# Normalised rows of a macaron layer: split on GpSimd and transposed by the DMA engines instead of TensorE, with two feed-forward layers a step earlier

## What is computed

```python
def ffn(x):                      # weights are +1 or -1, from boolean tables
    h = concat([x, -x])          # 256
    h = 2 * relu(s0 * h @ w(k0)) # 512
    h = 2 * relu(s1 * h @ w(k1)) # 512
    return s2 * h @ w(k2)        # 128

def attn(x):                     # 16 heads of 8
    q, k, v = x @ Wq.T + bq, x @ Wk.T + bk, x @ Wv.T + bv
    ctx = softmax(q @ k.T / sqrt(8)) @ v
    return layernorm(ctx + x) * gamma + beta

x = x + 0.5 * ffn(ln(x))
x = x + attn(ln(x))
x = x + 0.5 * ffn(ln(x))
```

## Time and profile before

| | us |
|---|---|
| median of three runs | 745.43 (744.24 to 748.4) |
| profiled execution, its own time | 745.53 |
| span from first to last instruction | 743.7 |

### The profile page before, as it was taken

How to read it: one execution, slowest core, us unless ns; L and a number is a source line. 1 busy time by engine, 2 the same in 40 slices (tenths; PEclk the granted TensorE clock), 3 DMA queues, 4 the chain that set the end, 5 groups by cost and what they waited for, 6 DMA issues and landing times.

```text
span 743.7 us, 18698 instructions
## 1 busy us (share of the span) xinstructions
PE 695.9 (94%) x7347; PEld 336.0 (45%) x7347; DVE 649.1 (87%) x1270; ACT 510.4 (69%) x745; POOL 365.9 (49%) x650
## 2 busy tenths in 40 slices
PE   7878999999999999999999999999999998787887
PEld 3434344544444454444444444444445444342346
DVE  6687898989999899999989898999989898887766
ACT  3426777777777777777787777767777776766644
POOL 6532455574454647454463746445465745254330
PEclk9999999999999999999999999999999999999999
DMA  3101010201102020201102020110201001010000
GB/s 82 57 15 52 16 53 2 65 17 45 37 3 66 17 66 16 67 17 29 39 16 66 16 66 17 44 38 2 67 17 65 17 33 36 30 38 2 11 7 30
DMA packets 29527, 25.65 MB, mean 34 GB/s; under 512 B 4353, under 2 KB 29441, under 8 KB 29441
## 3 DMA queue, kind: packets, MB, share of 16 engines
q1 hardware_dynamic: 27824, 23.74, 10.0%
q10 hardware_dynamic: 1616, 0.72, 0.3%
HBM read 5.05 MB, written 4.19 MB: 12 GB/s over the span
## 4 chain that ended last, share of the span: by engine, by line
PE 70%; DVE 20%; issue 4%; ACT 3%; POOL 2%; DMA 1%; SPq 0%; DVEq 0%; POOLq 0%
PE ps_c L876 15%; PE ps_z L702 13%; PE ps_z L703 11%; DVE row_max L1507 9%; PE ps_s L823 9%; DVE ffn_lo L1382 6%; PE ps_z L692 3%; PE ps_z L693 3%; PE ps_z L684 2%; PE ps_m L808 2%; PE ps_m L797 2%; ACT ffn_hi L1117 2%; PE ps_c L797 2%; PE ps_z L713 2%; DVE k_lo L1498 1%
## 5 line engine op out<-in xcount | busy, mean ns | idle before, releaser
L1507 DVE TENSOR_REDUCE row_max<-ps_s 128x4 f32<-128x1024 f32 x256 | 312.3, 1220 | 31.0 <-PE ps_s L823 29.3
L1156 ACT ACTIVATE probs<-ps_t,score_scale 128x1024 f32<-128x1024 f32 x252 | 280.2, 1112 | 62.2 <-PE ps_t L836 59.6
L1117 ACT ACTIVATE ffn_hi<-ps_z 128x512 f16<-128x512 f32 x261 | 149.8, 595 | 80.1 <-PE ps_z L703 63.2
L702 PE MATMUL ps_z<-ffn_hi,w 128*128 128x512 f16 x464 | 177.1, 382 | 0.8
L703 PE MATMUL ps_z<-ffn_lo,w 128*128 128x512 f16 x464 | 175.9, 379 | 0.0
L1382 DVE SCALAR_TENSOR_TENSOR ffn_lo<-ps_z,ffn_hi 128x512 f16<-128x512 f32 x232 | 154.3, 684 | 20.3 <-ACT ffn_hi L1117 17.4
L876 PE MATMUL ps_c<-probs,v_cols 128*32 128x256 f32 x2048 | 131.9, 386 | 1.3 <-ACT probs L1156 0.7
L823 PE MATMUL ps_s<-k_rows,q_rows 32*128 32x256 f16 x1024 | 100.2, 273 | 14.8 <-DVE row_max L1507 12.7
L836 PE MATMUL ps_t<-q_rows,k_rows 32*128 32x256 f16 x992 | 97.1, 273 | 0.0
L876 PEld LDWEIGHTS ps_c<-probs,v_cols 128*32 128x32 f32 x2048 | 57.0, 109 | 54.3 <-issue 26.6
L823 PEld LDWEIGHTS ps_s<-k_rows,q_rows 32*128 32x128 f16 x1024 | 29.0, 92 | 103.8 <-issue 50.4
(11 more groups left out here) (223 smaller groups left out, 1101.6 us busy)
## 6 DMA issues: line engine op xcount, KB each, us to landing
x<-L_attn_x SPq DMA_DIRECT2D x16, 256.0 KB, 2.7
q_rows<-q_hi SPq DMA_DIRECT2D x32, 128.0 KB, 2.5
k_rows<-k_hi SPq DMA_DIRECT2D x31, 128.0 KB, 2.1
y<-x SPq DMA_DIRECT2D x15, 256.0 KB, 2.2
q_rows<-no_max SPq DMA_DIRECT2D x16, 128.0 KB, 2.2
q_rows<-q_lo SPq DMA_DIRECT2D x16, 128.0 KB, 2.2
k_rows<-k_lo SPq DMA_DIRECT2D x15, 128.0 KB, 2.1
q_rows<-max_rows SPq DMA_DIRECT2D x64, 8.0 KB
```

Of the source, the lines that this page charges most:

```text
L702: pe.matmul(o[:], w, ffn_hi[:, 1 + k, :], start=(k == 0), stop=False)
L1117: a_.activation(ffn_hi[:, use, :], ps_z[use % 2][:], ACT.Relu if use else ACT.Copy, scale=1.0 if use else XN_SCALE).then_inc(z_hi, 1)
L1156: a_.activation(probs[n % PROBS][:, j:j + 2, :], o[:], ACT.Exp, scale=score_scale[:, 0:1]).then_inc(s_exp, 1)
L1507: v.tensor_reduce(row_max[hb % 2][:].rearrange("p (a l) e -> p l a e", a=2)[:, j:j + 2, :, g % 2], ps_s[:].rearrange("p l (a k) -> p l a k ...
```

## The change

The rows of 26 feed-forwards (all but feed-forward 0 and those of the last two iterations; the solo ones stay as well) and of the attention of tiles 1 to 15 are no longer transposed by TensorE. GpSimd multiplies the centred rows by a scaled factor twice, once to half precision and once to full, subtracts, and so has the `hi` and the `lo` rows side by side in `ffn_rows` or `att_rows` (128 partitions x 1024 half-precision elements, 256 KB). SP issues one transposing transfer to `ffn_cols` or `att_cols`. These feed-forwards have nine uses of `ps_z` instead of ten, and their pieces of the first and middle layer stand one step earlier; the last layer keeps its steps. The query projection goes from step 8 to 11, the key projection from 11 to 13. Statistics of `ffn_a` are finished at step 7 instead of 10, those of `next_b` at 26 instead of 27, those of the attention at 27 instead of 26. `tail_base` follows the first `split_max` instead of preceding it.

```diff
-AT = {"LNT": 6, "Q": 8, "K": 11, "CT0": 14, "CT1": 22, "V": 25}
+AT = {"Q": 11, "K": 13, "CT0": 14, "CT1": 22, "V": 25}
-AT_STATS_A, AT_STATS_B, AT_STATS_PREP = ((2, 2, 9, 9), 10), ((24, 24, 25, 25), 27), ((18, 18, 20, 20), 26)
+AT_STATS_A, AT_STATS_B, AT_STATS_PREP = ((2, 2, 6, 6), 7), ((24, 24, 25, 25), 26), ((18, 18, 20, 20), 27)
...
+FFN_IN_SOON = {1: 0, 2: 1, 3: 2, 4: 3}
+FFN_MID_SOON = tuple((5 + n, 2 * n, 2 * n + 2) for n in range(8))
+FFN_MID_DONE_SOON = {6: 0, 8: 1, 10: 2, 12: 3}
...
+        FFNS_ON_PE = (0, second_ffn(T - 4), second_ffn(T - 3))
+
+        def by_dma(f):
+
+            return f not in FFNS_ON_PE
...
+            def turn_ffn(f):
+
+                sp.wait_ge(z_full, z_use(f - 1, 5))
+                sp.wait_ge(f_xn, f + 1)
+                sp.dma_start_transpose(ffn_cols[:], ffn_rows[:].rearrange("p i d -> p (i d)")).then_inc(s_cols, 16)
+
+            def turn_att(it):
+
+                sp.wait_ge(m_full, it.misc["Q"])
+                sp.wait_ge(a_xn, it.t + 2)
+                sp.dma_start_transpose(att_cols[:].rearrange("p (i n) -> p i n", n=P),
+                                       att_rows[:].rearrange("p i d -> p (i d)")).then_inc(s_att_cols, 16)
+
             def steps(it):
...
                 if it.prev:
                     place_max(t - 1, 1 - par, 3)
+                if it.prep and it.prev:
+                    turn_att(it)
                 if it.cur and it.prev:
                     place_max(t, par, 0)
+                if it.first and it.prev:
+                    turn_ffn(it.next_b)
+                elif it.stats_a and by_dma(it.ffn_a):
+                    turn_ffn(it.ffn_a)
                 if not it.prev:
-                    sp.wait_ge(z_free, Z_USES)
+                    turn_ffn(it.ffn_b)
+                    sp.wait_ge(z_free, z_before(1))
...
                 if it.cur:
                     place_max(t, par, 2)
+                if it.next_b is not None and (not it.first or not it.prev):
+                    turn_ffn(it.next_b)
...
+            def ffn_rows_norm(f, src):
+
+                k = rs_steps(f)
+                pool.wait_ge(f_mv, f + 1)
+                g.tensor_tensor(ffn_ve[:], ffn_mv[:, :, 1], eps[:], ALU.add).then_inc(f_rs, 1)
+                g.tensor_tensor(ffn_xc[:], src[:], ffn_mv[:, :, 0:1].broadcast_to([P, TT, P]), ALU.subtract)
+                pool.wait_ge(f_rs, k + 1)
+                g.tensor_tensor(ffn_rs[:], ffn_ve[:], minus_half[:], ALU.pow).then_inc(f_rs, 1)
+                pool.wait_ge(f_rs, k + 2)
+                g.tensor_tensor(ffn_rs_fit[:], ffn_rs[:], xn_scale[:], ALU.mult).then_inc(f_rs, 1)
+                pool.wait_ge(f_rs, k + 3)
+                if by_dma(f - 1):
+                    pool.wait_ge(s_cols, cols_landed(f - 1))
+                else:
+                    pool.wait_ge(z_full, z_use(f - 1, 0) + 1)
+                fit = ffn_rs_fit[:].unsqueeze(2).broadcast_to([P, TT, P])
+                g.tensor_tensor(ffn_rows[:, 0:TT, :], ffn_xc[:], fit, ALU.mult)
+                g.tensor_tensor(ffn_xn[:], ffn_xc[:], fit, ALU.mult).then_inc(f_rs, 1)
+                pool.wait_ge(f_rs, k + 4)
+                g.tensor_tensor(ffn_rows[:, TT:2 * TT, :], ffn_xn[:], ffn_rows[:, 0:TT, :], ALU.subtract).then_inc(f_xn, 1)
...
             def att_norm(t, par):
...
+                g.tensor_tensor(att_rows[:, 0:TT, :], att_xc[:], fit, ALU.mult)
+                g.tensor_tensor(att_xs[:], att_xc[:], fit, ALU.mult).then_inc(a_rs, 1)
+                pool.wait_ge(a_rs, k + 4)
+                g.tensor_tensor(att_rows[:, TT:2 * TT, :], att_xs[:], att_rows[:, 0:TT, :], ALU.subtract).then_inc(a_xn, 1)
+                g.tensor_tensor(att_xn[par][:], att_xc[:], att_rs[:].unsqueeze(2).broadcast_to([P, TT, P]),
+                                ALU.mult).then_inc(a_base, 1)
...
                 if alone:
                     ffn_deviation(it.ffn_a)
-                elif it.prev:
-                    tail_base(t, par)
                 split_max(t, 0)
-                if alone:
+                if it.prev:
                     tail_base(t, par)
...
             def ffn_in(f, m):
                 if f == 0 and m == 0:
                     pe.wait_ge(q_lo[SOLO_FIRST], Z_USES)
-                pe.wait_ge(z_free, Z_USES * f + 1 + max(0, m - 1))
-                o = bank_of(1 + m)
-                pe.matmul(o[:], w0[:, m * P:(m + 1) * P], ffn_hi[:, 0, :], start=True, stop=False)
-                pe.matmul(o[:], w0[:, m * P:(m + 1) * P], ffn_lo[:, 0, :], start=False, stop=True).then_inc(z_full, 1)
+                if by_dma(f) and m == 0:
+                    pe.wait_ge(s_cols, cols_landed(f))
+                pe.wait_ge(z_free, z_use(f, 1 + m) - 1 + (m == 0 and not by_dma(f)))
+                o = z_bank(f, 1 + m)
+                pe.matmul(o[:], w0[:, m * P:(m + 1) * P], ffn_cols[:, 0:TT, :], start=True, stop=False)
+                pe.matmul(o[:], w0[:, m * P:(m + 1) * P], ffn_cols[:, TT:2 * TT, :], start=False,
+                          stop=True).then_inc(z_full, 1)
...
                     if it.prep:
-                        if s == at(it, "LNT"):
-                            att_transpose(t + 1, 1 - par, it.misc["LNT"])
                         if s == at(it, "V"):
                             project_v(it.misc["V"])
...
                         if s == at(it, "Q"):
+                            pe.wait_ge(s_att_cols, 16 * (t + 1))
                             project(0, it.misc["Q"])
```

More of the change, by code:

```diff
@@ L680, in ffn_transpose @@
                     pe.wait_ge(q_lo[SOLO_FIRST], 5)
[L681 removed]
+                at_least(pe, z_free, z_before(f) - 1)
                 pe.wait_ge(f_xn, f + 1)
                 for i in range(TT):
[L684 removed]
+                    last = pe.transpose(z_bank(f, 0)[:, i * P:(i + 1) * P], ffn_xn[:, i, :], ident[:])
                 last.then_inc(z_full, 1)
@@ L720, in ffn_piece @@
             def ffn_piece(f, s):
-                if s == 0:
+                if s == 0 and not by_dma(f):
                     ffn_transpose(f)
-                elif s in FFN_IN:
-                    ffn_in(f, FFN_IN[s])
-                for at, lo, hi in FFN_MID:
+                elif s in ffn_in_at(f):
+                    ffn_in(f, ffn_in_at(f)[s])
+                for at, lo, hi in ffn_mid_at(f):
                     if s == at:
@@ L1398, in ffn_piece @@
             def ffn_piece(f, s, src, dst, stored=None, based=None):
-                if s == 0:
+                if s == 0 and not by_dma(f):
                     z_rest(f, 0)
-                elif s in FFN_IN:
-                    z_rest(f, 1 + FFN_IN[s])
-                elif s in FFN_MID_DONE:
-                    z_rest(f, 5 + FFN_MID_DONE[s])
+                elif s in ffn_in_at(f):
+                    z_rest(f, 1 + ffn_in_at(f)[s])
+                elif s in ffn_mid_done(f):
+                    z_rest(f, 5 + ffn_mid_done(f)[s])
                 elif s == FFN_RESIDUAL:
@@ L1440, in ffn_apply @@
             def ffn_apply(f, src):
-                dve.wait_ge(f_rs, 2 * f + 2)
-                at_least(dve, z_full, Z_USES * f - (Z_USES - 1))
+                dve.wait_ge(f_rs, rs_steps(f) + 2)
+                dve.wait_ge(f_xn, f)
+                if not by_dma(f - 1):
+                    dve.wait_ge(z_full, z_use(f - 1, 0) + 1)
                 scale_rows(ffn_xn, src, ffn_mv, ffn_rs, TT).then_inc(f_xn, 1)
@@ L1594, in steps @@
                     pieces = ffn_work(it, s - 1)
-                    maxima_first = any(piece in FFN_MID_DONE for _, _, piece in pieces)
+                    maxima_first = any(piece in ffn_mid_done(f) for f, _, piece in pieces)
                     if maxima_first and it.cur and s % 2 == 0:
```

158 lines of the change are left out of this document (96 added, 62 removed).

## The result

| | before | after |
|---|---|---|
| median of 4 runs, us | 744.84 (744.24 to 748.4) | 776.32 (775.17 to 778.31) |
| profiled execution, us | 745.53 | 775.17 |
| its span, us; mean granted clock | 743.7; 0.998 | 773.4; 0.987 |

The changed kernel takes 1.0415 times as long, 95% interval 1.0374 to 1.0457: 31.5 us more, where I had forecast 14.6 more (760.0 us). The time lies inside the range of 734 to 790, on the side that I held likeliest, and still inside the forecast's own 749 to 780, near its top; but the loss is more than twice the one forecast.

What follows compares the result with a forecast made beforehand. TensorE, busy 94%, was taken to bound the kernel; after the change, a loop through GpSimd's norm and the transfer. Period 44.1, 1.4 more, twelve times 16.5: 745.5 + 16.5 - 2 = 760 us; range 734 to 790, forecast's own 749 to 780.

Steps and rivals of the forecast that it cites:

- Columns late at step 1: At TensorE's first layer, columns land 8.0 + D after step 26's scores, wanted at 8.6 to 8.8 us; TensorE waits about D.
- GpSimd's norm: On GpSimd, from start to end of a feed-forward's norm: 5.9 us (5.7 to 6.1), where it was 3.3.
- one is paid, not two: Second half of the tile, step 17: its wait has the same debt, 39.9 + D, and hangs on the same GpSimd start.
- The two stalls ahead of the last layer: TensorE at each feed-forward's end: 0.37 and 0.63 us waiting for VectorE's rest should go, 1.0 us per iteration.
- period = constant + D: Loop through step 26, GpSimd's norm and the transfer: period 31.8 + 8.0 + D = 39.8 + D.
- D: Transposing transfer's time from issue to landing: taken as 4.3 us, bounds 2.1 to 4.8.
- if nothing were late: One loop iteration without late inputs: 42.73 less 1.8 of transposes and 1.0 of stalls, 39.9 us.
- 31.8 us from step 1 to step 26: TensorE's loop stretch: 32.55 us less transposes 0.63 and 0.59 and stall 0.37, plus 0.86 for one middle-layer piece.
- Rival A: Transposing transfer as fast as a plain one: D 2.1 to 2.7, period 41.9 to 42.5, 738 us; taken as faster, 0.22.
- Rival B: Queue pushes the transpose block by block: D = 6.8, period 46.6, whole 790 us; B or longer, 0.14.
- Rival C: GpSimd not late, chain a us shorter: 748 us with D = 4.3; shares 0.14 with D of 2.9 to 3.4.
- Outside the loop: Outside the twelve iterations: five groups of transposes leave at 0.6 us each, of which 2 us kept as gain.

Runs made afterwards that it cites:

- f0: Changed kernel with no transfer of the feed-forwards' rows (TensorE reads them untransposed) and a plain transfer of the attention's: 741.99 us, ratio 0.9951, period 42.37.
- s1: s0 with the first layer's third block behind the context, on TensorE and ScalarE alike: 753.39 us, ratio 1.0110, period 42.85.
- b2: b1 with the third block behind the context product of its step: 775.59 us, ratio 1.0390, period 44.34.
- b1: Kernel before, transposes still on TensorE, only the first two layers of each feed-forward one step sooner: 786.34 us, ratio 1.0533, period 45.33.
- s7: s0 with the feed-forward's layers back at their old steps: 748.76 us, ratio 1.0053, period 42.93.
- f1: s0 with rows padded by 16 elements, so copies go in 256-byte pieces: 771.75 us, ratio 1.0351, transfer 2.9 us, period 44.38.
- s0: Changed kernel with both transposing transfers made plain copies, rows left untransposed: 765.95 us, ratio 1.0273, transfer 2.4 us, period 43.85.
- s6: s0 with the next feed-forward's statistics at steps 20, 21 and 23 and the third block behind the context: 743.15 us, ratio 0.9967.
- s3: s6 with GpSimd's product and bias for the tail's base moved behind the second feed-forward's rows: 740.69 us, ratio 0.9919, period 41.98.

## Why the prediction was right in direction and too small

**Right.** Columns late at step 1 in every tile, TensorE waiting in order behind them; GpSimd's norm at 5.82 us (forecast 5.9, though its own terms add up to 6.0; the difference of two full tiles took 1.17, between the bounds of 1.04 and 1.28); GpSimd's start 2.27 us after step 26's scores (2.1 forecast); step 17's columns in time, "one is paid, not two": issued at 361.44 and used at 365.33 without a wait. Inside the loop TensorE never waited for the attention's columns, nor for any other transfer than `ffn_cols`. The two stalls ahead of the last layer are gone, and VectorE's share fell to 84% of the period. Above all the form "period = constant + D": three transfers confirm it. TensorE's wait was forecast as about D and is 2.3 us. The 39.9 "if nothing were late" was too low: TensorE alone is busy 40.4 us a tile, f0 without a transfer took 42.37, and the shortest period of all runs is 41.98.

**The term of the loop that failed: 31.8 us from step 1 to step 26.** It measured 33.26. I took the earlier trace rows and subtracted the transposes and stalls, but put at nothing what the earlier step does to the alternation of the two PSUM banks. It moves the third block to piece 3, ahead of the context, where its bank is still being read; s1 and b2 each gain 1.0 us a tile by moving it back, b1 has the stall with the transposes still there, and s7 without the shift has not. The other 0.5 of the 1.46 us is not placed. My reading that the chain leaves TensorE only at the end of each feed-forward was not whole either: in the kernel before it also does at 313.91, for `ffn_hi` (0.61 us) and `ffn_lo` (0.70). The stall takes the place of the two last-layer stalls that I had booked as a gain of 1.0 us. A stall at one bank had left and another had come, a rival that the prediction did not name. At 1.46 us a tile this term is 17.5 us of the twelve iterations, more than the whole loss that I forecast; the error in D took most of it back.

**D, 4.3 forecast, 3.1 measured**, inside the bounds of 2.1 to 4.8. The small pieces of `k1` and `k2` were the wrong likeness: they are not transfers from SBUF to SBUF, which took 2.9 us in 256-byte pieces (f1) and 2.4 in whole rows (s0). The two errors nearly cancelled in the period (44.55 measured, 44.1 forecast), and that is luck. So is part of the direction: with D = 3.1 the prediction's own sum gives a period of 42.9 and 745.5 us, which is no change.

**Rival A** had the transfer nearly right and the result wrong. I had put break-even at D = 2.9; with 41.45 it lies at 1.3, below every transfer of this size in these traces. s0 is rival A built: 2.4 us, and still 766 us instead of 738. The Trainium skill ("Advanced Engine Details and Errata", X-Bar Transpose) says of the transposes that they "are as fast as regular DMAs"; here the transposing one took 3.1 us and the regular one 2.4, so not quite, and the measurement decides. The Trainium skill's 1309 ns for one block ("VectorE: DVE Perf Modes", The three transpose paths) does not add up over blocks: eight blocks landed in 3.1 us, not in 10.5; one block alone was not run. **Rival B** is out by the same 3.1 us. **Rival C** is out too: GpSimd was 0.2 us later than forecast.

**Outside the loop: -2 forecast, about +8 measured** (5.6 ahead and 2.4 behind). This is the term that missed by most. Up to 163 us TensorE's matmuls wait 3.5 us for `ffn_cols` (2.93 of them at 82.39, for a transfer that took 4.3), 1.4 for `att_cols` and 1.6 for the bank, and one stretch at half clock falls there; I had counted only the transposes that leave. In the tail stand a wait of 2.65 us for GpSimd's `max_parts` at 660.50, which the kernel before has not, and 6.8 us at half clock instead of 3.4. How the 8 us divide over these was not tried. The stretches at half clock, which I did not have, cost in the loop too: the three iterations in which one falls took 1.1, 1.5 and 0.9 us more than the others. s0, whose waits are shorter, had as much of them (20.4 us) as after, and f1 with longer waits than s0 had 17.0; s1, with the same wait for columns as s0, had 10.2, and so had f0, without any such wait, two thirds of it in the tail. So their number does not follow the length of the wait. Which iterations are hit stays open.

Together: ten iterations at 1.82 us are 18.2, the half-clock stretches in three of them 3.5 more, the eleventh nothing, and 8.0 outside make the 29.7 us of span. The forecast had 16.5 for the loop, nothing for the clock and -2 outside: of the 15 us that it was too small by, 10 lie outside the loop, 3.5 are the clock's, and only the small remainder is the loop's, because its two errors cancelled there.

## What to carry to other kernels

Taking work off the fullest engine gives time only if its input comes back no later than before; write the loop as "from the consumer's start round to the consumer's start" and sum it before counting what is saved. When pieces that share two alternating PSUM banks are moved by a step, write out anew which block meets which bank, and what stands between the two. Give the iterations outside the loop a sum of their own. And start the producer's chain sooner before asking for its result sooner: with the statistics three steps earlier and the third block back behind its context, the same parts run in 743 us instead of 766 (plain transfers), which is 0.3% under the kernel before, and 0.8% with GpSimd's order mended as well. Beyond that the chain points to VectorE's row maxima, which was not tried.

## What the runs showed of the hardware that I had not expected

- A transposing transfer of 256 KB of 16-bit elements from SBUF to SBUF landed 3.1 us after its issue (26 of them, 3.0 to 4.3), against 2.4 for a plain one and 2.9 for one in 256-byte pieces. Its issue holds SP's queue 1.27 us, where the plain one holds it 0.50. With it 47648 of 72821 packets are under 512 bytes, where the kernel before had 4353 of 29527 and f1, with its 256-byte pieces, 46992 of 72165; so 256 bytes is my estimate of the piece.
- Single plain transfers of that size landed after 4.2 to 4.5 us where most took 2.3 (s6, s3). Without room for them they cost 1.7 to 1.9 us of a tile, with 2.3 us of room nothing.
- On GpSimd a difference of a float32 and a float16 tile of 128x512 took 1.17 us, against 1.28 for two float32 tiles.
- A TensorE that waited 2.3 us for columns once a tile and was busy 40.4 of 44.55 us was granted its lower clock in three of eleven iterations, for 3.4 us each: the mean clock was 0.987, where it had been 0.998. s0 with waits of 1.6 us also had 0.987, s1 with the same waits 0.993; what decides it stays open.
